# Four-layer graph network on one core: loops written out, half of the sums between the products, one-hot rows made a group ahead

## What is computed

```
layer 0: out = clip(h + segsum(h[src]*edge_weight*w0, dst) + h*slw, 0, 1)
layer 1: out = segsum(sum_k t[:,k] * (h[dst] @ W[k]), src)      16 basis products of two hat functions of edge_attr_2
layer 2: out = concat over both directions of segsum(einsum(relu(LN(h))[ends], edge_attr_8 @ We + be)) + relu(LN(h)) @ Wr + b
layer 3: agg = segsum(silu(einsum(h[dst], edge_attr_8, Wmsg)) @ Wmlin, src);  out = h + silu(einsum(h, agg, Wupd)) @ Wulin
x = x + out after each layer
```

## Time and profile before

| | |
|---|---|
| median of 3 runs | 4584.79 us |
| the profiled execution | 4580.59 us, of which span 4578.8 us |
| busy: DVE, POOL, PE, ACT | 2888.0 (63%), 2834.2 (62%), 2142.2 (47%), 1181.5 us (26%) |
| mean granted clock of PE | 0.716 of full |
| instructions recorded | 36295 |
| edge parts, about | layer 0: 630 to 1220, layer 1: 1735 to 2550, layer 2: 2700 to 3446, layer 3: 3560 to 4156 |
| update | 4160 to 4578 |

### The profile page before, as it was taken

One profiled execution on the slowest core, in us unless ns is written; L12 is line 12 of the kernel. 1 busy time (PEld: TensorE's weight loads), 2 busy tenths in 40 slices (PEclk: granted clock), 3 DMA queues, 4 the chain that ended last, 5 costly groups with the idle time before them and its releaser, 6 DMA issues.

```text
span 4578.8 us, 36295 instructions
## 1 busy us (share of the span) xinstructions
PE 2142.2 (47%) x6770; PEld 1442.9 (32%) x6770; DVE 2888.0 (63%) x4329; ACT 1181.5 (26%) x2942; POOL 2834.2 (62%) x2799
## 2 busy tenths in 40 slices
PE   1200015555200005666666126666660566666998
PEld 0100014444200003333333115555550344433444
DVE  8890026666460006777777777777776688876887
ACT  1010013333310003333333234444341344431111
POOL 4877777777777776555554036555530677773776
PEclk7555557777655557888888657777775788888999
DMA  6010013333530002222224212222243233352110
GB/s 167 7 47 24 8 38 105 110 104 111 83 97 5 5 5 52 72 72 72 72 72 71 90 63 85 83 84 76 83 80 114 82 108 100 106 84 65 32 32 24
DMA packets 200402, 319.82 MB, mean 70 GB/s; under 512 B 83898, under 2 KB 166698, under 8 KB 199971
## 3 DMA queue, kind: packets, MB, share of 16 engines
q1 hardware_dynamic: 112848, 265.61, 16.3%
q0 software_dynamic: 82368, 21.64, 7.5%
q10 hardware_dynamic: 5140, 32.09, 1.8%
HBM read 66.90 MB, written 252.21 MB: 70 GB/s over the span
## 4 chain that ended last, share of the span: by engine, by line
PE 22%; DVE 19%; issue 10%; POOL 6%; DMA 2%; SPq 2%; DVEq 1%; ACT 0%; POOLq 0%
DVE work L1122 9%; PE psX L562 8%; PE psX L651 7%; POOL rows L464 5%; PE psK L553 4%; DVE psX L1152 2%; PE psX L578 2%; DVE natD L1147 2%; DMA rows<-table,rec 1%; DVEq L1122 1%; DVE work L1104 1%; SPq L407 1%; SPq L408 1%; PE psK L628 1%; DVE at_hi L1099 1%
## 5 line engine op out<-in xcount | busy, mean ns | idle before, releaser
L464 POOL DMA_INDIRECT rows<-table,rec x1792 | 1692.6, 945 | 1268.0 <-issue 528.4
L553 PE MATMUL psK<-work 128*128 128x224 f32 x3584 | 927.7, 424 | 648.8 <-DVE work L1104 374.4
L553 PEld LDWEIGHTS psK<-work 128*128 128x128 f32 x3584 | 848.1, 241 | 819.3 <-issue 501.8
L1122 DVE SCALAR_TENSOR_TENSOR work<-work,keep,psK 128x224 f32<-128x224 f32 x1792 | 799.8, 446 | 233.7 <-DVE work L1122 45.2
L562 PE MATMUL psX<-natD 128*128 128x512 f32 (+1 forms) x1120 | 682.7, 750 | 535.6 <-DVE natD L1147 257.2
L749 ACT ACTIVATE work<-iota,rec 128x128 f32<-128x128 f32 x1792 | 546.0, 391 | 641.3 <-PE psK L553 360.2
L446 POOL DMA_INDIRECT edges_by_dst<-natD,pos x391 | 440.4, 1126 | 184.1 <-issue 126.7
L562 PEld LDWEIGHTS psX<-natD 128*128 128x128 f32 x1120 | 258.0, 254 | 800.1 <-DVE natD L1147 329.7
L446 POOL DMA_INDIRECT edges_by_src<-natS,pos x391 | 403.5, 1032 | 127.2 <-issue 127.2
L1104 DVE TENSOR_TENSOR work<-at_hi,psX 128x1792 f32<-128x1792 f32 x224 | 452.3, 2019 | 6.1 <-ACT psX L791 0.3
L589 PE MATMUL psX<-ident,rows 128*128 128x128 f32 x168 | 51.9, 309 | 803.9 <-DMA rows<-table,rec 803.9
(11 more groups left out here) (142 smaller groups left out, 2068.0 us busy)
## 6 DMA issues: line engine op xcount, KB each, us to landing
scan<-work SPq DMA_DIRECT2D x224, 896.0 KB, 3.6
rows<-table,rec POOLq DMA_INDIRECT x1792
table<-h ACTq DMA_DIRECT2D x28, 896.0 KB, 3.6
work<-scan SPq DMA_DIRECT2D x168, 112.0 KB, 2.0
rec<-edges_by_dst SPq DMA_DIRECT2D x112, 84.0 KB, 1.9
natD<-scan SPq DMA_DIRECT2D x56, 112.0 KB, 2.0
edges_by_dst<-natD,pos POOLq DMA_INDIRECT x391, 2.1
edges_by_src<-natS,pos POOLq DMA_INDIRECT x391
```

Source lines behind the costliest of these rows:

```text
L464: pool.indirect_dma_start(out=rows[k][:, u * D:(u + 1) * D], out_offset=None, in_=table.ap(), in_offset=bass.IndirectOffsetOnAxis(ap=rec[k ...
L553: nc.tensor.matmul(psK[:, o:o + BW], at_lo[par][:, t * P:(t + 1) * P], spread[par][:, t * BW:(t + 1) * BW], start=True, stop=True)\
L1122: V.scalar_tensor_tensor(acc[par][:, t * BW:(t + 1) * BW], was, keep[s][:, bass.ds(q * G + t, 1)], psK[:, o:o + BW], ALU.mult, ALU.add).th ...
```

## The change

1. All `Fori` loops become Python loops, that is, written-out instructions with constant waits (edge rounds on all five engines, the SP loop over the 8 loads of a chunk, the update). The bare semaphore increments `pool_go` and `sp_go` go.
2. On PE the first half of the preceding group's sums stands behind products 0 and 1, then come the rest of the products and the root products, then the second half. In layers 0 and 3 the order on PE is as before.
3. On ACT `partition_of` is called for group g+1 at the end of group g (behind the silu in layer 3), so it stands ahead of `features` of group g+1, and waits for the sums of group g-1.

```diff
@@ block.sync @@
-                    with sp.Fori(0, ROUNDS - 2) as i:
+                    for i in range(0, ROUNDS - 2):
...
-                        with sp.Fori(0, PER) as j:
+                        for j in range(0, PER):
@@ block.gpsimd @@
                     pool.wait_ge(rec_in[k], i * 16 + (PAST_REC[l] + 16))
-                    pool.sem_inc(pool_go, 1)
...
-                with pool.Fori(1, ROUNDS) as i:
+                for i in range(1, ROUNDS):
@@ block.tensor @@
                         pe.wait_ge(e["bandS"], g + 1)
-                        for m in range(n):
+                        for m in range(2):
                             product(i, k, m, first)
-                        if l == 2:
-                            root_products(i, k, first)
                     if not first:
                         sums(i, k, 0, second)
+                    for m in range(2, n):
+                        product(i, k, m, first)
+                    if l == 2:
+                        root_products(i, k, first)
+                    if not first:
                         sums(i, k, 1, second)
...
-                with pe.Fori(1, ROUNDS) as i:
+                for i in range(1, ROUNDS):
@@ block.scalar @@
                 def partition_of(i, k, started):
                     par = k % 2
+                    act.wait_ge(rec_in[k], i * 16 + (PAST_REC[l] + 16))
                     if started:
                         act.wait_ge(e["summed"], i * (RING * G) + (k - 1) * G)
...
-                def group(i, k, started=True):
+                def group(i, k, started=True, last_one=False):
+
                     if l == 2 and k == 0:
                         root_rows(i, k)
                     if l:
                         features(i, k)
-                    act.wait_ge(rec_in[k], i * 16 + (PAST_REC[l] + 16))
                     if l == 1:
                         hat_factors(i, k)
-                    partition_of(i, k, started)
                     if l == 3:
                         act.wait_ge(e["preact"], i * RING + (k + 1))
                         S.activation(raw[k % 2], basis, ACT.Silu, scale=NORM_MSG).then_inc(e["silu"], 1)
-
+                    if last_one:
+                        return
+                    if k + 1 < RING:
+                        partition_of(i, k + 1, started)
+                    else:
+                        partition_of(i + 1, 0, True)
+
+                partition_of(0, 0, False)
                 for k in range(RING):
-                    group(0, k, k >= 2)
-                with act.Fori(1, ROUNDS) as i:
+                    group(0, k, k >= 1)
+                for i in range(1, ROUNDS - 1):
                     for k in range(RING):
                         group(i, k)
+                for k in range(RING):
+                    group(ROUNDS - 1, k, last_one=k == RING - 1)
@@ block.vector @@
-                with dve.Fori(1, ROUNDS) as i:
+                for i in range(1, ROUNDS):
...
```

More of the change, by code:

```diff
@@ L229, in build_gnn @@
         stored = sem("stored")
-        pool_go = sem("pool_go")
-        sp_go = sem("sp_go")
         dve_step = sem("dve_step")
@@ L379, in refill @@
                         sp.wait_ge(e["spread"], g + 1)
-                        sp.sem_inc(sp_go, 1)
                         sp.wait_ge(e["lo"], g + 1)
@@ L499, in _ @@
             update(0, True)
-            with pool.Fori(1, NCH) as c:
+            for c in range(1, NCH):
                 update(c, False)
@@ L656, in _ @@
             step(0, True, False)
-            with pe.Fori(1, NCH - 1) as c:
+            for c in range(1, NCH - 1):
                 step(c, False, False)
@@ L867, in _ @@
             step(0, True, False)
-            with act.Fori(1, NCH - 1) as c:
+            for c in range(1, NCH - 1):
                 step(c, False, False)
@@ L1269, in _ @@
             update(0, True)
-            with dve.Fori(1, NCH) as c:
+            for c in range(1, NCH):
                 update(c, False)
```

## The result

| | |
|---|---|
| changed kernel | 4570.89 us median of 11 runs (4566.51 to 4572.95) |
| kernel before, same chip | 4583.71 us median of 11 runs (4573.70 to 4586.45) |
| ratio | 0.9974, 95% interval 0.9965 to 0.9984 |
| profiled execution | span 4571.2 us (before 4578.8), mean granted clock 0.701 (before 0.716) |

A forecast was written before the change was run, and what follows sets the result against it. POOL's issue bounds layers 0 and 3, PE at half clock delays layer 1, SP's loads the node parts; a new PE-ACT loop then rules layers 1 to 3. -80 + 5 + 51 + 11 - 40 = -53: 4530 us, 80% range 4400 to 4640.

The forecast's parts named there:

- The new loop: Layers 1 to 3: sums, one-hot rows, features, products, sums close a loop; 4.1 us of it without PE in layer 1.
- I take 1.9: PE's restart at half clock after its idle gap adds 1.9 us to each group of layers 1 to 3.
- PE's part at full clock is 5.26 us: Layer 3: PE's work in a group, product 0 to last sum, takes 5.26 us at 2.4 GHz.
- The sum's form: Layers 1 to 3: group time is gap plus PE's full-clock work plus restart, 12.97, 13.09 and 11.26 us.
- rival (a): Cold restarts: 2.58 us extra in all three layers, each 0.1 us costing 16.4 us; 4640 us, slower; chance 0.2.
- It is not counted a second time: Layer 1: writing out saves about 0.6 us a group of VectorE's register work, not added since the loop rules.
- rival (d): The reordering does nothing; only written-out code and loads count, about 4525 us; chance 0.05.
- POOL's straight code, +11: Layer 0: written-out gathers bring four stalls of 3.0 us in place of 0.3, 11 us more.
- SP's loads, -40: Node parts and update: written-out loads save 0.33 us each, 96 loads plus 8 us, 40 us less.
- Rival (b), warm restarts, 4335: PE's gap too short to drop the clock; layer 1 at 11.9 us, layer 3 at POOL's pace; 4335 us; chance 0.1.
- What would show it: Signs: paces 12.9, 13.1, 11.3 in layers 1 to 3, PE idle 4.1 us, POOL stalls, loads 1.2 us apart.

The follow-up runs named there:

- act_only_b: Changed kernel with PE's old order (all products, then all sums), one-hot rows still a group ahead: 4564.19 us, ratio 0.9968 to the kernel before.
- three_buffers_b: Changed kernel with a third buffer of one-hot rows in layers 1 to 3, both reorderings kept: 4359.40 us, ratio 0.9519 to the kernel before.
- pe_filler: Changed kernel with 12 unread matmuls on PE ahead of each transpose of layers 1 and 3: 4450.85 us, ratio 0.9722 to the kernel before.
- act_gap1: Changed kernel with one more ACT copy between the one-hot rows and the next features, layers 1 to 3: 4584.57 us, ratio 1.0012.
- act_gap3: Changed kernel with three more ACT copies between the one-hot rows and the next features, layers 1 to 3: 4624.32 us, ratio 1.0097.
- loops_kept: Kernel before with both reorderings put in and its counted loops kept: 4605.47 us, ratio 1.0056 to the kernel before.
- unroll_only_b: Changed kernel with PE's and ACT's old orders, loops written out: 4444.73 us, ratio 0.9711; without _b, the same on the slow chip, ratio 0.9743.
- pe_only: Changed kernel with ACT's old order, PE's half of the sums between the products: ratio 0.9683 on the slow chip; run again, 4356.75 us, 0.9513.

## Why the prediction was wrong in size

The direction, the loop and its place were right; the sum was not. By its own steps:

- *The new loop.* Right in kind. The gap was 3.94 for 4.1 us, and the wait is there once a group. `act_only_b` shows that ACT's move closes it, and `three_buffers_b` that a buffer opens it.
- *"I take 1.9".* **This is the step that failed**: one extra for three layers, chosen between rows 4 and 5. In the forecast's own terms it was 9.70 - 6.97 = 2.73 us in layer 1. In layer 2 the four groups of a round last 8.92, 9.05, 8.67 and 8.66 us, against 6.32 at full clock: 2.5 in the mean. In layer 3 it was 10.86 - 3.94 - 5.26 = 1.66. With them layer 1 gave 42 us for 80, layer 2 cost 34 for 5, and layer 3 cost 29 for 51: together +20 us where the text had -24.
- *"PE's part at full clock is 5.26 us".* Too long by 0.25, which with a gap 0.16 shorter makes the 0.40 us by which layer 3 came out below its 11.26. Windows from product 0 to the last sum, of layers 1 and 2 of the changed kernel, and of layer 3 of `pe_filler`:

```profile
2009.06:2018.76 9.70, 9.70 (x25) 6.25 (x25) 6.96 (x15) 1.11 (x5) 6.12 (x7) 0.69 0.33 105
3016.07:3025.12 9.05, 9.05 (x34) 7.76 (x34) 5.34 (x12) 1.06 (x3) 6.92 (x8) 0.67 0.32 108
...
3705.71:3710.72 5.01, 5.01 (x20) 3.70 (x20) 3.58 (x6) 0.28 (x1) 3.79 (x5) 1.00 0.58 200
```

  The same 20 records as in rows 4 take 5.01 us. Length times (1 - granted clock) estimates what half clock cost: 9.70 x 0.31 = 3.0 us in layer 1, 9.05 x 0.33 = 3.0 in layer 2 (2.9 in the mean of the four groups), and 10.86 - 3.94 - 5.01 = 1.9 in layer 3. So 1.9 was right for layer 3 and 1.0 to 1.1 short in layers 1 and 2, and PE's work was taken some 0.3 too long in all three. The forecast's rows already said so: 7.84 x 0.37 = 2.9 for rows 5, and 7.61 x 0.35 and 6.54 x 0.24 both leave 5.0 us of work. Rows 5 were misread too: they start at product 2 (1778.20, behind a wait of PE of 3.47 us), not at product 0, and PE waits for nothing inside them. Their 2.58 was clock alone, and the better guide for layers 1 and 2.
- *The sum's form.* The text added gap, work and restart as if they were free of each other, and rival (a) and its 16.4 us for each 0.1 us rest on that. `act_gap1` and `act_gap3` show that they aren't: in layers 1 and 2 a longer gap is given back by a shorter half-clock part, in layer 3 it costs more than itself. The page TensorE: Matmul & The Clock Gate of the Trainium skill, under HAM oscillation, says that each burst after an idle stretch restarts at half rate; the trace agrees in layer 1 (granted clock 0.50 from 2009.06 to 2012.84), but not in every group of layer 3, where the products behind the same gap take 3.78 us in one group (from 3712.14) and 2.81 in the next (from 3724.15). That the pace then no longer answers to small changes of the gap stands only in these runs.
- *"It is not counted a second time".* Right inside the loop (`loops_kept`: 31 us are all that the counted loops cost). But layer 2 and layer 3 without the loop were never priced: rival (d) put writing out alone at 4525, and `unroll_only_b` took 4445, 135 us below the kernel before: 45 in layer 1, 49 in layer 2, 10 in layer 3, 4 in layer 0 and some 30 outside them. So the small total hides large parts: 223 us are gained and 215 given back.
- *POOL's straight code, +11.* Wrong. The changed kernel's waits of POOL in layer 0 (660 to 1200 us) have no stall over 0.3 us, as many as before, and layer 0 kept its pace:

```profile
POOL rows L459 <- issue: 129.5, 425, 0.3
```

  The 3 us stalls of rows 7 belong to the placement and not to straight code as such; what makes them stays open. The page Runtime: NRT & Kernel Launch of the Trainium skill, Instruction fetch mechanics, says that crossing a block is mostly hidden. For the gathers the trace agrees with it, against my reading.
- *SP's loads, -40.* -28.6 came. The saving of each load is 0.38 for the 0.33 taken. Advanced Engine Details and Errata of the Trainium skill, Control Flow Timing, gives about 108 ns for a compare-and-branch; a whole turn of this loop cost 0.38 us. What failed is the count: the 56 loads ahead of layer 1 were not on the path, since POOL's placement ends there last (it makes 72.5% of the chain from 1200 to 1750 us, no load is in it, and the stretch went from 542.0 to 544.0 us).
- *Rival (b), warm restarts, 4335.* Its state is what the matmuls of `pe_filler` bring about: layer 1 at 12.07 where the text had 11.9, layer 3 at 10.2. It did not happen by itself.
- *What would show it.* POOL did not stall, loads were 1.1 us apart, POOL waited for records in layer 3 (39.5 us), and the wait of PE was where the text put it. VectorE's wait for product 2 was 2.2 us (0.17 for product 3), not under 1: with products 0 and 1 at half clock ahead of it, product 2 comes late. Layer 3 at 10.9 and layer 1 at 13.6 lay inside its own limits of 10 and 14, so those limits were too wide to catch the error.

## What to carry to other kernels

Before work is made a group ahead, count its buffers: with two, "a group ahead" means "behind the last reader of the group before", and if the next consumer's input stands behind that work in the same in-order engine, a loop closes that no engine's busy share shows. To size what a half clock costs, multiply a stretch's length by 1 minus its granted clock; subtracting two stretches also subtracts their waits. Try each part of such a change alone; here the parts were worth -135, -88 and +215 us. Where PE idles once in each group at a cost in clock, cheap matmuls into a free part of PSUM, placed where PE waits anyway, can give more than they take (-120 and -63 us here).

## What the runs showed of the hardware

- A pace held by the clock: layer 1 has 13.65 us in most groups with three different orders of work, and a gap longer by 0.59 us moves it by nothing (13.65 still, the mean 13.62 for 13.61). In layer 3, with less work in a group, the same 0.59 us cost 0.93.
- PE's added 2.84 us a group took 1.54 us off each group of layer 1 (13.61 to 12.07).
- One chip ran the same kernel 11% slower (5101 us for 4580) and the time lay in the edge parts (layer 0 took 855 us in `unroll_only`, 558 in `unroll_only_b`). Ratios between kernels on it had the right order, but the steps between them were smaller: `pe_only` was 0.6% below `unroll_only` there and 2.0% on the other.
